# Causal attention stage: the 384-column and 128-column key-row scores share a PSUM slot, and the maxima are turned two pieces later

## The chip, the cores and the metric

The kernel runs on one core of a Trainium2 chip. Its time is the device time of one execution in microseconds (us); the median of the runs is what is compared. Five engines work beside one another, each through its own list of instructions in order: TensorE (PE, with its weight loads PEld), VectorE (DVE), ScalarE (ACT), GpSimd (POOL) and SyncE (SP, which only starts transfers here). Semaphores tie them together.

## The reference, cut to what matters

Two transformer layers run one after the other on x of shape (4, 1024, 128). The change touches only the attention of the second layer: 16 heads of 8, causal, with a recurrence beside it.

```python
scores = jnp.einsum('bhid,bhjd->bhij', q, k) * scale
causal_mask = jnp.triu(jnp.full((Ll, Ll), -10000.0, dtype=scores.dtype), 1)
attn = jax.nn.softmax(scores + causal_mask, axis=-1)
y_softmax = jnp.einsum('bhij,bhjd->bhid', attn, v)
...
state = retention * state + Gamma * hebbian          # the recurrence, one step per position
y_t = jnp.einsum('bhij,bhj->bhi', W_static + state, q_t)
...
y = alpha * y_softmax + (1.0 - alpha) * y_stp
```

## The kernel before

The causal stage works on 4 batches times 4 groups of 4 heads: 16 units `(b, g)`. The 1024 positions are 8 tiles of P = 128; BANK is 512 columns, one PSUM bank. A `ring` of three PSUM slots of two banks each (1024 columns) takes nearly every result of TensorE. Slots go round in the order of the items, and PE may fill one only when the item three before it has been read (`pe_wait_free`).

Each unit is computed in two passes.

- **M items (row maxima).** For each tile of queries, PE makes the scores with the queries on the partitions (L1280, and two small masking matmuls L1284 and L1287 where the tile is on the diagonal), and DVE reduces them to negated maxima (L1430). A unit has 20 such pieces. After the last one DVE joins two halves (L1434), and POOL splits the maxima into three bf16 parts with four small instructions (L1678, L1680, L1682, L1684).
- **S item (turned maxima).** PE transposes the parts (L1294) into a ring slot, ACT copies them (L1517), and SP starts four small transfers (L1606) that put them as extra rows under the queries, so that the key-row scores come out with the maximum already subtracted.
- **W items (key-row scores).** PE makes the scores with the keys on the partitions (L1309, masks L1313 and L1316), and ACT takes their exponential (L1530) from the ring slot into one of four buffers `c_probs`.
- **V items.** PE multiplies the exponentials by the values (L1337) into the accumulator `acc`, which is no ring slot. ACT copies it out at the end of a chunk (A item, L1536).

W and V go through `KEY_STEPS`: chunk c = 0 of 512 queries needs key tiles j = 0 to 3, chunk c = 1 needs j = 0 to 7. The last four tiles of a chunk lie on the diagonal, and leave 512, 384, 256 and 128 columns of queries. `score_pairs` says how the two pairs of heads share slots: a step of 512 or 384 columns takes two slots, one for each pair; a step of 256 or 128 columns takes one slot for both pairs. So a chunk takes 6 or 14 slots, a unit 20, the stage 320, with 320 exponentials: 14 of 1024 columns in a unit, 4 of 768 and 2 of 512.

`causal_order` writes the common order of all items. It keeps a model of when PE, ACT, DVE and the slots come free. M pieces of the next unit (`ahead`) are put before W and V items so that they lead by 9 to 19 W items, at a rate `ratio` = 21/20 of them (20 M and one S) to each W; they may be put earlier when the model says that this costs no wait. V of a step is put after the W items of the next step. The recurrence is a chain of side items, tied to the key steps (8 rounds j in a batch, 6 key steps for each): `kv` (POOL L1691), `scan` (DVE L1440), `scale` (ACT L1543), `read` (POOL L1703 and L1706). The preparation of the next batch and the finishing of the last one (`turn`, `q`, `k`, `v`, `gate1`, `gate2`, `vT`, `beta`, `att`, `tp`) are side items too; 19 of them a batch take ring slots.

Of the kernel before, what the change touches and what calls it, by code (L numbers as in the profile page):

```python
# [8 lines left out]
ACT = mybir.ActivationFunctionType  # L9
# [4 lines left out]
P = 128  # L14
# [106 lines left out]
def build(nc, x_in, packed, x_out, place, batches, T, known):  # L121
# [7 lines left out]
    with ctx:  # L129
# [764 lines left out]

        def score_pairs(c, j):
            cols = (c + 1) * BANK - max(c * BANK, j * P)
            return [(0, 1)] if 2 * cols <= BANK else [(0,), (1,)]

        KEY_STEPS = [(c, j) for c in range(HALVES) for j in range((c + 1) * BANK // P)]

# [111 lines left out]
        def causal_order():  # L1012
# [64 lines left out]
            def times(item):  # L1077
                if item[0] == "next":
                    return MOE_TIMES.get(item[1], (0, (("D", 1.1),), 0))
                if item[0] == "M":  # L1080
                    n, (_, a, c, _, per) = item[3], causal_pieces(item[3])[item[4]]
                    mask = 0.15 * per if c == (n + 1) * P else 0
                    return 0.00077 * per * (c - a) + mask, (("D", 0.16 + 0.00204 * per * (c - a)),), 1
                if item[0] in "WV":
                    c, j = item[3:5]
                    a = max(c * BANK, j * P)
                    cols = (c + 1) * BANK - a
                    if item[0] == "V":
                        return 0.00205 * cols, (), 0
                    n = len(score_pairs(c, j)[item[5]])  # L1090
                    return n * (0.00077 * cols + (0.15 if a == j * P else 0)), (("A", 0.17 + 0.00166 * n * cols),), 1
                return TIMES.get(item[0], (0, (), 0))
# [5 lines left out]
            def begin(item):  # L1098
                t = clock["P"]
                if times(item)[2]:  # L1100
                    t = max(t, free[0])
                return max(t, made[item[1:]]) if item[0] == "V" else t

            def put(item):
# [12 lines left out]
                if item[0] == "W":  # L1117
                    made[item[1:5]] = done + HOP

# [25 lines left out]
            for u in units:  # L1145
                for k, (c, j) in enumerate(KEY_STEPS):
                    for i in range(len(score_pairs(c, j))):
                        put_ahead(("W", *u, c, j, i))
                        put(("W", *u, c, j, i))
                        done += 1  # L1150
                        while sums:
                            put(sums.pop())

                    late.append(("V", *u, c, j))
                    if len(late) > 1:
                        item = late.pop(0)
                        put_ahead(item)
                        put(item)
                        if item[4] == (item[3] + 1) * BANK // P - 1:
                            sums.append(("A", *item[1:4]))  # L1160
# [14 lines left out]
        def causal():  # L1175
# [9 lines left out]
            chunk = lambda b, g, c: (b * GROUPS + g) * HALVES + c  # L1185
            first_query = lambda c, j: max(c * BANK, j * P)
            last_W = lambda b, g: ("W", b, g, *KEY_STEPS[-1], len(score_pairs(*KEY_STEPS[-1])) - 1)
            unit = lambda b, g: b * GROUPS + g
# [33 lines left out]
            def pe_program():  # L1222
# [3 lines left out]
                for item in order:  # L1226
# [70 lines left out]
                    elif kind == "W":  # L1297
# [3 lines left out]
                        pe.wait_ge(shift_signal(b, g, part), (b, g, part))  # L1301
                        a = first_query(c, j)
                        cols = (c + 1) * BANK - a
                        qs, ks = cq_stack[b % 2], ck_stack[b % 2]
                        diag = a == j * P
                        for k, pair in enumerate(score_pairs(c, j)[i]):
                            o = [ps[:, r * BANK + k * BANK // 2:r * BANK + k * BANK // 2 + cols] for r in range(2)]
                            for r in range(2):
                                mm = nc.tensor.matmul(o[r], ks[half(r, SHIFT), 2 * g + pair, j * P:(j + 1) * P],  # L1309
                                                      qs[half(r, SHIFT), 2 * g + pair, a:a + cols], start=True, stop=not diag)  # L1310
# [8 lines left out]
                    elif kind == "V":  # L1319
# [7 lines left out]
                        if j == 0 and ci >= 2:  # L1327
                            pe.wait_ge(c_copied, ci - 2)
                        shares = score_pairs(c, j)
                        pe.wait_ge(c_weights_made, ("W", *item[1:], len(shares) - 1))  # L1330
                        for i in range(2):
                            k = i if len(shares) > 1 else 0
                            weights = c_probs[w_index["W", b, g, c, j, k] % 4]
                            for r in range(2):
                                h = 2 * i + r
                                first = r * BANK + (i - k) * BANK // 2
                                mm = nc.tensor.matmul(  # L1337
                                    acc[ci % 2][32 * h:32 * h + HD + 1, a - c * BANK:BANK],
                                    c_values[b % 2][:, j, r * HEADS // 2 + 2 * g + i, :],
                                    weights[:, first:first + (c + 1) * BANK - a],  # L1340
                                    start=j == 0, stop=j == (c + 1) * BANK // P - 1, skip_group_check=True)
                        mm.then_inc(c_weighed.up(item), 1)
# [128 lines left out]
            def act_program():  # L1471
# [3 lines left out]
                for item in order:  # L1475
# [43 lines left out]
                    elif kind == "W":  # L1519
                        _, b, g, c, j, i = item  # L1520
                        wi = w_index[item]
                        cols = (c + 1) * BANK - first_query(c, j)
                        if len(score_pairs(c, j)) > 1:
                            view = lambda ap: ap[:, :].rearrange("p (r c) -> p r c", r=2)[:, :, 0:cols]
                        else:
                            view = lambda ap: ap[:, :].rearrange("p (r k c) -> p r k c", r=2, k=2)[:, :, :, 0:cols]
                        ac.wait_ge(c_key_scored, item)
                        if wi >= 4:
                            ac.wait_ge(c_weighed, ("V", *w_items[wi - 4][1:5]))
                        nc.scalar.activation(view(c_probs[wi % 4]), view(ps), ACT.Exp).then_inc(c_weights_made.up(item), 1)  # L1530
                    elif kind == "A":
                        _, b, g, c = item
                        ac.wait_ge(c_weighed, ("V", b, g, c, (c + 1) * BANK // P - 1))
                        if b:
# [1335 lines left out]
```

## Time and profile before

| | |
|---|---|
| median of 3 runs | 1893.22 us (1888.89 to 1899.77) |
| the profiled execution | 1901.14 us, span 1899.8 us |
| causal stage in it | from about 1030 to 1650 us of the span |
| busy in the stretch 1030 to 1650 | PE 505, DVE 483, ACT 404, POOL 319 us of 620 |
| pieces in the stage | 320 M, 320 W |

Each row of such a profile is one engine's busy time or one group of instructions. A bracket behind a row of the timeline is the time for which that engine sat idle before the instruction, and what ended it. PE's busy time has the latency of each matmul in it, so it is an upper value.

### The profile page before, as it was taken

How to read it: one execution, taken by the hardware profiler on the slowest of the kernel's cores; microseconds unless marked ns; L12 is line 12 of the kernel's file. 1: busy time of each engine (PE TensorE's matmuls, PEld its weight loads, DVE VectorE, ACT ScalarE, POOL GpSimd, SP SyncE). 2: the span in 40 equal slices, each digit the busy share in tenths (PEclk: the TensorE clock that was granted, in tenths of full speed). 3: DMA queues.
4: the chain of work that ended last, by engine and by line, in shares of the span. 5: the costliest groups of instructions: out<-in, count | busy, mean ns of one | idle time of the engine just before them, and what ended most of it. 6: DMA issues, size and time to landing. Idle time of an engine off the chain costs nothing. (4 is left out here: it accounts for less than half of the span.)

```text
span 1899.8 us, 45062 instructions
## 1 busy us (share of the span) xinstructions
PE 1656.2 (87%) x19472; PEld 1024.8 (54%) x19472; DVE 1276.2 (67%) x2059; ACT 1114.6 (59%) x1654; POOL 695.8 (37%) x508
## 2 busy tenths in 40 slices
PE   4588888999999999999997778888888888899999
PEld 2355555677677767776775233343343343466665
DVE  4566645667666666666765868877877886755664
ACT  2265567766676667667763366667766767533221
POOL 5212202444244434424443164555554564411100
PEclk7699898999999999999998699999998999999999
DMA  7674100000000000000014236236327323000000
GB/s 171 161 194 121 22 14 2 2 2 2 1 2 2 2 1 2 2 2 1 2 46 115 68 121 168 68 91 162 74 71 182 75 62 75 23 6 12 6 12 12
DMA packets 38748, 102.27 MB, mean 54 GB/s; under 512 B 3944, under 2 KB 12288, under 8 KB 35284
## 3 DMA queue, kind: packets, MB, share of 16 engines
q1 hardware_dynamic: 38548, 99.38, 20.6%
q8 instruction: 153, 2.51, 0.6%
q14 instruction: 47, 0.39, 0.1%
HBM read 67.12 MB, written 31.46 MB: 52 GB/s over the span
## 5 line engine op out<-in xcount | busy, mean ns | idle before, releaser
L1430 DVE TENSOR_REDUCE arena<-ring 128x2 f32<-128x1024 f32 (+2 forms) x320 | 342.1, 1110 | 87.8 <-PE ring L1287 61.9
L1530 ACT ACTIVATE arena<-ring 128x1024 f32<-128x1024 f32 (+1 forms) x320 | 291.2, 937 | 132.4 <-PE ring L1316 89.1
L1337 PE MATMUL accs<-arena 128*9 128x512 f32 (+3 forms) x1536 | 173.9, 526 | 2.7 <-ACT arena L1530 2.6
L1280 PE MATMUL ring<-arena 48*128 48x512 bf16 (+3 forms) x768 | 129.5, 349 | 40.7 <-DVE arena L1430 19.9
L1309 PE MATMUL ring<-arena 51*128 51x512 bf16 (+3 forms) x768 | 125.0, 344 | 45.4 <-DVE arena L1430 25.1
L2469 POOL TENSOR_TENSOR arena<-arena 128x1280 f32<-128x1280 f32 x28 | 65.3, 2332 | 266.6 <-PE accs L2239 235.2
L2453 POOL TENSOR_TENSOR arena<-arena 128x1024 f32<-128x1024 f32 x32 | 76.0, 2376 | 203.3 <-DVE arena L2329 203.3
L2461 POOL TENSOR_TENSOR arena<-arena 128x512 f32<-128x512 f32 x112 | 141.9, 1299 | 11.3 <-DVE arena L2310 11.3
L292 POOL TENSOR_SCALAR xn<-x,moments,rstd 128x128 f32<-128x128 f32 x88 | 70.5, 815 | 192.4 <-DVE rstd L263 174.2
L2736 ACT ACTIVATE arena<-ring 128x512 f32<-128x512 f32 x80 | 47.7, 597 | 147.3 <-PE ring L2591 140.5
L2696 DVE TENSOR_TENSOR arena<-arena,ring 128x512 f32<-128x512 f32 x80 | 55.0, 687 | 87.8 <-PE ring L2593 74.4
L1703 POOL TENSOR_TENSOR arena<-arena 128x1024 f32<-128x1024 f32 x28 | 65.9, 2353 | 128.6 <-ACT arena L1543 104.3
L1309 PEld LDWEIGHTS ring<-arena 51*128 51x128 bf16 x768 | 36.6, 95 | 138.9 <-DVE arena L1430 75.4
L2613 PEld LDWEIGHTS accs<-weights_large,arena 128*128 128x128 f32 x640 | 83.5, 192 | 27.1 <-issue 23.5
L2329 DVE TENSOR_TENSOR arena<-ring,arena 128x1024 f32<-128x1024 f32 x32 | 39.2, 1225 | 86.7 <-PE ring L2201 86.7
L1280 PEld LDWEIGHTS ring<-arena 48*128 48x128 bf16 x768 | 38.5, 96 | 109.1 <-DVE arena L1430 41.4
L623 DVE TENSOR_REDUCE arena<-ring 128x8 f32<-128x1024 f32 x51 | 61.7, 1220 | 46.3 <-PE ring L516 45.9
L2201 PE MATMUL ring<-arena 64*128 64x128 f32 x1024 | 91.1, 285 | 1.2 <-DVE arena L1955 1.1
L2003 ACT ACTIVATE arena<-ring 128x1024 f32<-128x1024 f32 x32 | 32.8, 1024 | 101.0 <-PE ring L1907 97.4
L2201 PEld LDWEIGHTS ring<-arena 64*128 64x128 f32 x1024 | 78.6, 187 | 21.8 <-issue 13.5
L2613 PE MATMUL accs<-weights_large,arena 128*128 128x128 f32 x640 | 84.5, 275 | 0.5 <-DVE arena L2701 0.5
L2413 ACT ACTIVATE arena<-arena 128x512 f32<-128x512 f32 x128 | 81.5, 707 | 0.0
(345 smaller groups left out, 4275.3 us busy)
## 6 DMA issues: line engine op xcount, KB each, us to landing
arena<-whole_k SPq DMA_DIRECT2D x32, 512.0 KB, 4.7
arena<-whole_q SPq DMA_DIRECT2D x32, 512.0 KB, 6.3
arena<-a_scratch_q SPq DMA_DIRECT2D x16, 384.0 KB, 7.3
arena<-a_scratch_k SPq DMA_DIRECT2D x16, 384.0 KB, 8.8
arena<-c_scratch_q SPq DMA_DIRECT2D x14, 384.0 KB, 8.0
arena<-c_scratch_k SPq DMA_DIRECT2D x14, 384.0 KB, 11.5
a_scratch_k<-arena SPq DMA_DIRECT2D x8, 512.0 KB, 4.1
c_scratch_k<-arena SPq DMA_DIRECT2D x8, 512.0 KB, 4.1
```

Of the source, the lines that this page charges most:

```text
L292: nc.gpsimd.tensor_scalar(xn[n % 4][:, :], x[:, b * NT + n, :], moments[:, n, 0:1], rstd[:, 3, n:n + 1], ALU.subtract, ALU.mult).then_inc( ...
L1280: mm = nc.tensor.matmul(o[r], qs[half(r, SCORE), pair, n * P:(n + 1) * P], ks[half(r, SCORE), pair, a:c], start=True, stop=not diag)
L1309: mm = nc.tensor.matmul(o[r], ks[half(r, SHIFT), 2 * g + pair, j * P:(j + 1) * P], qs[half(r, SHIFT), 2 * g + pair, a:a + cols], start=Tru ...
L1337: mm = nc.tensor.matmul(acc[ci % 2][32 * h:32 * h + HD + 1, a - c * BANK:BANK], c_values[b % 2][:, j, r * HEADS // 2 + 2 * g + i, :], weig ...
L1430: nc.vector.tensor_reduce(dst, src, AX.X, ALU.max, negate=True).then_inc(c_max_taken.up(item), 1)
L1530: nc.scalar.activation(view(c_probs[wi % 4]), view(ps), ACT.Exp).then_inc(c_weights_made.up(item), 1)
L1703: nc.gpsimd.tensor_tensor(sq[:, :], sk[:, :], sq[:, :], ALU.mult).then_inc(c_y_step.up((b, j)), 1)
L2201: mm = nc.tensor.matmul(ps[:, r * BANK + p * P:r * BANK + (p + 1) * P], k_[t % 2][half(r), p * P:(p + 1) * P], q_[t % 2][half(r), p * P:(p ...
L2413: nc.scalar.activation(v5[t % 2][:, 1 + r, :], v5[t % 2][:, 0, :], ACT.Copy, scale=route_hot[t // NT % 2][:, t % NT, r:r + 1]).then_inc(v_ ...
L2453: nc.gpsimd.tensor_tensor(masked[0][:, :], masked[0][:, :], masked[1][:, :], ALU.add).then_inc(gla_joined.up(t), 1)
L2461: nc.gpsimd.tensor_tensor(pair_cols(q2m[t % 2][:, r, :]), pair_cols(q2[t % 2][:, :]), hot_b[:, r * P:(r + 1) * P].unsqueeze(1).to_broadcas ...
L2613: mm = nc.tensor.matmul(moe_total[:, n * P:(n + 1) * P], hid[i % 3][:, n * P:(n + 1) * P], w("d_down", f * P, (f + 1) * P), start=f == 0 a ...
```

## The change

It touches three things.

- The scores of key tile `last - 3` (384 columns) and of the last key tile `last - 1` (128 columns) of a chunk go into the same slot, one slot for each pair of heads: 384 columns at 0 and 128 at 384 of each bank. The last key tile has no slot of its own any more. Every slot is full, so every exponential has 1024 columns. The matmuls and masks are the same as before.
- The steps of a chunk now go `..., last - 1, last - 2`. Step `last - 1` issues no W. Its V item follows V of `last - 3` directly, behind the W of `last - 2`, and V of `last - 2` comes last. Side items that were tied to the third and fourth step of a chunk's tail keep their step numbers.
- The S item is inserted after four M pieces of the next unit, not after two.

```diff
-        def score_pairs(c, j):
-            cols = (c + 1) * BANK - max(c * BANK, j * P)
-            return [(0, 1)] if 2 * cols <= BANK else [(0,), (1,)]
-        KEY_STEPS = [(c, j) for c in range(HALVES) for j in range((c + 1) * BANK // P)]
+        def chunk_steps(c):
+            last = (c + 1) * BANK // P
+            return [*range(last - 2), last - 1, last - 2]
+        KEY_STEPS = [(c, j) for c in range(HALVES) for j in chunk_steps(c)]
+        def score_blocks(c, j):
+            last = (c + 1) * BANK // P
+            if j == last - 1:
+                return []
+            if j == last - 2:
+                return [[(0, j, 0), (1, j, BANK // 2)]]
+            if j == last - 3:
+                return [[(pair, j, 0), (pair, last - 1, BANK - P)] for pair in range(2)]
+            return [[(pair, j, 0)] for pair in range(2)]
+        def blocks_of(c, j):
+            found = {pair: (step, i, a) for step in chunk_steps(c) for i, blocks in enumerate(score_blocks(c, step))
+                     for pair, tile, a in blocks if tile == j}
+            return [found[pair] for pair in range(2)]
...
-                    rows.insert(2, ("S", *units[u - 1], 0))
+                    rows.insert(4, ("S", *units[u - 1], 0))
...
-            ratio = (len(maxima(units[1])) + 1) / sum(len(score_pairs(*k)) for k in KEY_STEPS)
+            ratio = (len(maxima(units[1])) + 1) / sum(len(score_blocks(*k)) for k in KEY_STEPS)
...
-                    if len(late) > 1:
+                    while scores and len(late) > 1:
                         item = late.pop(0)
                         put_ahead(item)
                         put(item)
-                        if item[4] == (item[3] + 1) * BANK // P - 1:
+                        if item[4] == last_step(item[3]):
                             sums.append(("A", *item[1:4]))
...
-                        for k, pair in enumerate(score_pairs(c, j)[i]):
-                            o = [ps[:, r * BANK + k * BANK // 2:r * BANK + k * BANK // 2 + cols] for r in range(2)]
+                        for pair, tile, at in score_blocks(c, j)[i]:
+                            a = first_query(c, tile)
+                            cols = (c + 1) * BANK - a
+                            diag = a == tile * P
+                            o = [ps[:, r * BANK + at:r * BANK + at + cols] for r in range(2)]
...
-                            ac.wait_ge(c_weighed, ("V", *w_items[wi - 4][1:5]))
-                        nc.scalar.activation(view(c_probs[wi % 4]), view(ps), ACT.Exp).then_inc(c_weights_made.up(item), 1)
+                            *former, step, k = w_items[wi - 4][1:]
+                            ac.wait_ge(c_weighed, ("V", *former, score_blocks(former[2], step)[k][-1][1]))
+                        nc.scalar.activation(c_probs[wi % 4][:, :], ps[:, :], ACT.Exp).then_inc(c_weights_made.up(item), 1)
```

## Rows read from the trace of the kernel before

**Rows 1.** The page, busy time of each engine over the whole span.

```profile
PE 1656.2 (87%) x19472; PEld 1024.8 (54%) x19472; DVE 1276.2 (67%) x2059; ACT 1114.6 (59%) x1654; POOL 695.8 (37%) x508
```

**Rows 2.** Busy by stretch: length, then PE, PEld, DVE, ACT, POOL, clock, DMA share, GB/s.

```profile
1030.00:1650.00 620.00, 505.29 (x5750) 215.78 (x5751) 483.20 (x555) 404.19 (x472) 319.44 (x218) 0.93 0.39 99
...
1319.48:1348.41 28.93, 23.64 (x328) 8.93 (x328) 26.10 (x23) 22.16 (x26) 16.96 (x10) 1.00 0.37 89
...
1348.41:1391.95 43.54, 35.77 (x410) 17.02 (x412) 34.11 (x53) 28.95 (x34) 20.43 (x13) 1.00 0.21 50
```

**Rows 3.** The chain that ended last, by line, in the stretch 1093 to 1603.

```profile
by line: DVE arena L1430 24.0%; PE accs L1337 14.2%; DVE arena L1440 7.7%; issue 7.0%; PE ring L1309 6.0%; PE ring L1280 5.9%; ACT arena L1530 4.6%; PE ring L928 1.9%; POOL arena L1691 1.8%; PE ring L1348 1.8%; DMA c_scratch_q<-arena 1.5%; 
```

**Rows 4.** Groups by shape in 1030 to 1650: busy us, mean ns, idle before.

```profile
L1430 DVE TENSOR_REDUCE arena<-ring 128x2 f32<-128x1024 f32 x192 | 228.3, 1217 | 50.4 <-PE ring L1287 26.1 <-PE ring L1280 23.2
L1530 ACT ACTIVATE arena<-ring 128x1024 f32<-128x1024 f32 x224 | 222.4, 1022 | 100.9 <-PE ring L1316 58.5 <-PE ring L1309 41.9
...
L1530 ACT ACTIVATE arena<-ring 128x768 f32<-128x768 f32 x64 | 51.2, 812 | 17.2 <-PE ring L1316 16.7
...
L1530 ACT ACTIVATE arena<-ring 128x512 f32<-128x512 f32 x32 | 19.1, 595 | 14.3 <-PE ring L1316 13.9
```

**Rows 5.** Line L1430: what its engine sat idle for (us, times).

```profile
  PE ring L1287: 61.9, 60
  PE ring L1280: 23.2, 23
```

**Rows 6.** ACT timeline: three of the 15 full-width S copies.

```profile
1093.83 1.01 ACT L1517 ACTIVATE arena<-ring 12x1024 bf16<-12x1024 f32 x1 [1.33 <-PE ring L1294]
...
1199.63 1.01 ACT L1517 ACTIVATE arena<-ring 12x1024 bf16<-12x1024 f32 x1 [0.16 <-PE ring L1294]
...
1602.92 1.01 ACT L1517 ACTIVATE arena<-ring 12x1024 bf16<-12x1024 f32 x1 [1.57 <-PE ring L1294]
```

**Rows 7.** DVE timeline of a unit without side jobs, its idle gaps.

```profile
1470.15 0.96 DVE L1430 TENSOR_REDUCE arena<-ring 128x2 f32<-128x768 f32 x1 [0.52 <-PE ring L1287]
1471.70 5.54 DVE L1430 TENSOR_REDUCE arena<-ring 128x2 f32<-128x768 f32 x5 [0.59 <-PE ring L1287]
1477.91 1.82 DVE L1430 TENSOR_REDUCE arena<-ring 128x4 f32<-128x512 f32 x2 [0.68 <-PE ring L1287]
1480.48 3.49 DVE L1430 TENSOR_REDUCE arena<-ring 128x2 f32<-128x1024 f32 x3 [0.74 <-PE ring L1280]
```

**Rows 8.** POOL and DVE timeline around a split, and another unit's L1682.

```profile
1163.10 2.36 POOL L1691 TENSOR_TENSOR arena<-arena 128x1024 f32<-128x1024 f32 x1
...
1166.02 2.28 DVE L1440 TENSOR_TENSOR_SCAN arena<-arena 128x1024 f32<-128x1024 f32 x1
...
1166.19 2.14 POOL L1682 CAST arena<-arena 128x32 bf16<-128x32 f32 x1
...
1601.55 0.24 POOL L1682 CAST arena<-arena 128x32 bf16<-128x32 f32 x1
```

**Rows 9.** Line L1294 in 1080 to 1600: idle of PE until (us, times).

```profile
  POOL arena L1684: 4.3, 4
```

**Rows 10.** A slow stretch behind an S: busy by engine and clock, timeline.

```profile
1168.50:1173.00 4.50, 4.14 (x35) 1.40 (x37) 2.15 (x3) 4.00 (x5) 0.53 (x2) 0.65 0.51 128
...
1170.18 1.90 PE L1337 MATMUL accs<-arena 128*9 128x512 f32 x8
...
1172.71 5.54 DVE L1430 TENSOR_REDUCE arena<-ring 128x2 f32<-128x768 f32 x5 [1.82 <-PE ring L1287]
...
1175.39 1.05 PE L1337 MATMUL accs<-arena 128*9 128x512 f32 x8
```

**Rows 11.** PE timeline: V of 384 columns and V of 128 columns.

```profile
1184.82 0.83 PE L1337 MATMUL accs<-arena 128*9 128x384 f32 x8
...
1189.83 0.41 PE L1337 MATMUL accs<-arena 128*9 128x128 f32 x8
```

**Rows 12.** ACT timeline near the stage's end: the copy of turned beta.

```profile
1637.76 1.02 ACT L1507 ACTIVATE arena<-ring 128x1024 f32<-128x1024 f32 x1 [4.90 <-PE ring L1254]
```

More of the change, by code:

```diff
@@ L892, in stack_signal @@
             return ((c_stack_there[0, 0], (0, 0)), (c_stack_there[0, 1], (0, 1)), (c_stack_there[1, 0], (0, 2)))[min(g, 2)]
-        def score_pairs(c, j):
-            cols = (c + 1) * BANK - max(c * BANK, j * P)
-            return [(0, 1)] if 2 * cols <= BANK else [(0,), (1,)]
-        KEY_STEPS = [(c, j) for c in range(HALVES) for j in range((c + 1) * BANK // P)]
+        def chunk_steps(c):
+            last = (c + 1) * BANK // P
+            return [*range(last - 2), last - 1, last - 2]
+        KEY_STEPS = [(c, j) for c in range(HALVES) for j in chunk_steps(c)]
+        last_step = lambda c: chunk_steps(c)[-1]
+        first_query = lambda c, j: max(c * BANK, j * P)
+        def score_blocks(c, j):
[11 more added lines that the diff above has]
+            return [found[pair] for pair in range(2)]
         CAUSAL_FIRST = {
@@ L1083, in times @@
                     return 0.00077 * per * (c - a) + mask, (("D", 0.16 + 0.00204 * per * (c - a)),), 1
-                if item[0] in "WV":
+                if item[0] == "V":
                     c, j = item[3:5]
[L1086 to L1091, printed above, removed]
+                    return 0.00205 * ((c + 1) * BANK - first_query(c, j)), (), 0
+                if item[0] == "W":
+                    c, j, i = item[3:6]
+                    masks = sum(tile * P >= c * BANK for _, tile, _ in score_blocks(c, j)[i])
+                    return 0.00077 * BANK + 0.15 * masks, (("A", 0.17 + 0.00166 * BANK),), 1
                 return TIMES.get(item[0], (0, (), 0))
@@ L1101, in begin @@
                     t = max(t, free[0])
-                return max(t, made[item[1:]]) if item[0] == "V" else t
+                return max(t, *(made[item[1:4] + (step, i)] for step, i, _ in blocks_of(*item[3:5]))) if item[0] == "V" else t
             def put(item):
@@ L1117, in put @@
                 if item[0] == "W":
-                    made[item[1:5]] = done + HOP
+                    made[item[1:]] = done + HOP
             first, second = ([i for i in maxima(units[0]) if (i[3] < NT // 2) == early] for early in (True, False))
@@ L1146, in causal_order @@
                 for k, (c, j) in enumerate(KEY_STEPS):
-                    for i in range(len(score_pairs(c, j))):
+                    scores = score_blocks(c, j)
+                    for i in range(len(scores)):
                         put_ahead(("W", *u, c, j, i))
@@ L1185, in causal @@
             chunk = lambda b, g, c: (b * GROUPS + g) * HALVES + c
-            first_query = lambda c, j: max(c * BANK, j * P)
-            last_W = lambda b, g: ("W", b, g, *KEY_STEPS[-1], len(score_pairs(*KEY_STEPS[-1])) - 1)
+            last_W = lambda b, g: ("W", b, g, *KEY_STEPS[-1], len(score_blocks(*KEY_STEPS[-1])) - 1)
             unit = lambda b, g: b * GROUPS + g
@@ L1301, in pe_program @@
                         pe.wait_ge(shift_signal(b, g, part), (b, g, part))
-                        a = first_query(c, j)
-                        cols = (c + 1) * BANK - a
                         qs, ks = cq_stack[b % 2], ck_stack[b % 2]
-                        diag = a == j * P
-                        for k, pair in enumerate(score_pairs(c, j)[i]):
-                            o = [ps[:, r * BANK + k * BANK // 2:r * BANK + k * BANK // 2 + cols] for r in range(2)]
+                        for pair, tile, at in score_blocks(c, j)[i]:
[3 more added lines that the diff above has]
+                            o = [ps[:, r * BANK + at:r * BANK + at + cols] for r in range(2)]
                             for r in range(2):
-                                mm = nc.tensor.matmul(o[r], ks[half(r, SHIFT), 2 * g + pair, j * P:(j + 1) * P],
+                                mm = nc.tensor.matmul(o[r], ks[half(r, SHIFT), 2 * g + pair, tile * P:(tile + 1) * P],
                                                       qs[half(r, SHIFT), 2 * g + pair, a:a + cols], start=True, stop=not diag)
@@ L1328, in pe_program @@
                             pe.wait_ge(c_copied, ci - 2)
[L1329 to L1333, printed above, removed]
+                        for step, i, _ in blocks_of(c, j):
+                            pe.wait_ge(c_weights_made, ("W", b, g, c, step, i))
+                        for pair, (step, i, at) in enumerate(blocks_of(c, j)):
+                            weights = c_probs[w_index["W", b, g, c, step, i] % 4]
                             for r in range(2):
-                                h = 2 * i + r
-                                first = r * BANK + (i - k) * BANK // 2
+                                h = 2 * pair + r
+                                first = r * BANK + at
                                 mm = nc.tensor.matmul(
                                     acc[ci % 2][32 * h:32 * h + HD + 1, a - c * BANK:BANK],
-                                    c_values[b % 2][:, j, r * HEADS // 2 + 2 * g + i, :],
+                                    c_values[b % 2][:, j, r * HEADS // 2 + 2 * g + pair, :],
                                     weights[:, first:first + (c + 1) * BANK - a],
-                                    start=j == 0, stop=j == (c + 1) * BANK // P - 1, skip_group_check=True)
+                                    start=j == 0, stop=j == last_step(c), skip_group_check=True)
                         mm.then_inc(c_weighed.up(item), 1)
```

7 lines of the change are left out of this document (1 added, 6 removed).

## The prediction, made before the changed kernel was run

> **What bounds the kernel now.** I read the page first, then the stage by stretches, then the chain of waits inside it, and last the timelines of single units. Over the whole span PE is the busiest engine [rows 1], but that is an average over four layers of work; the change touches only the causal stage, so only the stage counts. There PE shows 505 us of 620 busy, DVE 483, ACT 404 [rows 2]. PE's share holds the latency of each matmul, so DVE is as near to its limit. The chain of waits agrees: of 510 us in the middle of the stage the row-max reductions take 24%, the V matmuls 14%, the scan 8%, and the exponential only 4.6% [rows 3].
>
> The reader is to see two kinds of unit. A plain unit, without side jobs, takes 28.93 us with DVE busy for 26.10 of them [rows 2]. Its gaps on DVE of over half a us are 0.52, 0.59, 0.68 and 0.74, together 2.53 us of the 2.8 that DVE has free [rows 7]; nothing can give more there than these. A unit with side jobs takes up to 43.54 us with DVE busy for 34.11 [rows 2]: no engine is full, and the three ring slots and the common order set the pace. Between the S copies at 1093.83 and 1602.92 [rows 6] lie 14 units; four are plain like the one at 1319, ten have side jobs. In front of its reductions DVE waits 85.1 us in all for scores, in 83 gaps [rows 5].
>
> **The W slots.** The change takes two of 20 W slots from each unit, 32 in all. PE has the same matmuls, masks and columns: nothing saved, nothing added. ACT loses two exponentials of 595 ns and makes four 210 ns longer (1022 against 812 ns) [rows 4]: 1190 less 840 is 350 ns a unit, 5.6 us over 16 units. ACT has a third of its time free, so these 5.6 us are not the gain by themselves. What may pay is the turn of the slot. I price a slot by time: from the S copy at 1199.63 to that at 1348.41 [rows 2, 6] a batch passes in 148.78 us. It has 4 times 41 ring pieces and 19 side pieces, 183 in all. Without its plain unit (28.93 us, 41 pieces) there are 119.85 us for 142 pieces, 0.84 us a slot. A removed slot's work does not vanish: it makes two others longer by 0.21 us of ACT each, 0.42 us. What is left is 0.42 us a slot, 0.85 a unit, 8.5 us in ten units. The bounds: below it 0, if DVE or the V matmuls fill every turn that comes free (a loss is the rivals' matter); above it the full price, 10 x 2 x 0.84 = 17 us.
>
> In the four plain units DVE sets the time. Here the removed slot helps PE and ACT, which already wait. Of the gaps, 0.52 and 0.59 follow the S piece, which takes one of three slots between two M pieces; they move with it. I take 0.4 us a unit out of the other 1.42, so 1.6 us; the bounds are 0 and 1.42 x 4 = 5.7.
>
> The first unit is a ramp and the last one ends on the recurrence: ACT waits 4.90 us for the turned beta [rows 12], and PE had to wait for POOL's round of the recurrence before that. Fewer exponentials don't shorten that round. I give both nothing; if that cover is gone, they give at most 0.85 each.
>
> **The S piece two later.** Fourteen S items move. PE waited at them for POOL's split 4 times, 4.3 us in all [rows 9]; that wait can go whole or not at all. In the unit at 1166 the split is slow because L1682 takes 2.14 us, where it takes 0.24 in the last unit: in the first case it runs beside DVE's scan of 2.28 us, and ends with it [rows 8]. The next reduction stands behind the same scan, so DVE would have been late anyway. So most of PE's wait is covered, and I take 1.4 of the 4.3 us; bounds 0 and 4.3. The clock is part of it: behind the S at 1168, where PE had stood still, the mean granted clock of 4.5 us is 0.65, so a good part of them ran at 1.2 instead of 2.4 GHz; one V group takes 1.90 us where 1.05 is usual, and DVE has a gap of 1.82 us [rows 10] where others have 0.59 [rows 7]. That is inside the 1.4.
>
> A rule speaks against this part. The Trainium skill (GPSIMD Engine Reference, section 8, Key points) says that POOL shares its SBUF interfaces with DVE and is held up by DVE instructions with two SBUF inputs; a scan is one. By that rule, the trace agrees (2.14 against 0.24 us). It makes the split end with the scan wherever S stands, so the moved S would be worth 0 and the sum 10.1 us instead of 11.5; by the bare row of PE's waits it would be 14.4.
>
> What is queued behind: on SP the four small transfers of S move back with it, by two M pieces, some 2.4 us; the fetches for the recurrence stand behind them, but they wait for POOL anyway. The W items that need S come over seven ring pieces after it, by the lead of nine W items; at 0.71 us a piece and the W and V between, they don't meet it. The other new wait, ACT's exponential on V of tile `last - 1`, is behind a V that PE has already passed when the buffer comes round.
>
> **The sum.** 8.5 + 1.6 + 1.4 = 11.5 us. The profiled execution took 1901.14 us with a span of 1899.8; it lies 7.9 us above the median, so I take the difference from both: 1889.6 us for this execution, 1881.7 us for the median, which I round to 1882.
>
> **Rivals.**
>
> *Nothing to gain.* DVE sets the pace in more than the plain units, and the turns that come free are filled by waiting. For it: DVE at 78% of the whole stage [rows 2] and 24% of the chain [rows 3]. Against: a gap in every third or fourth reduction [rows 5], and 9.4 us free in the long unit [rows 2]. Time: 1893.2 less 0 to 4, so 1891.
>
> *More than expected.* Each removed slot brings its full price, 17 us in ten units and 5.7 in the plain ones, and the S waits go: 4.3. That is 27 us, 1866. For it: ACT idles 14.3 us before 32 short exponentials and 100.9 before 224 full ones, 0.45 us each in both [rows 4], so a slot costs a turn whatever is in it. Against: DVE's 90% in plain units.
>
> *Slower: the scan comes too early.* The side items keep their step numbers, but a chunk's tail now has one W less. The scan of every second round stands in the tail of chunk 0, three steps after its `kv`. In the unit at 1163 POOL's `kv` ends at 1165.46 and the scan starts at 1166.02 [rows 8]: a slack of 0.56 us. Between scale and scan there were 6 W and, at 21/20, 6.3 M; now 5 W and, at 21/18, 5.8 M. If that moves the scan up by one reduction of 1.22 us, DVE stands for 0.66 us; over some 15 units 10 us, which eats the gain. That is where it decides. If it moves by two, it is 1.88 us each, 28 us, less 11.5: 1910; the middle of both is 1901 to 1902. Against it: the M pieces have lead enough, and half a piece is less than the slack.
>
> *The order is worse by chance.* V of 384 and V of 128 columns now run together, 0.83 + 0.41 = 1.24 us [rows 11] in which PE fills no slot, about one reduction of 1.22 [rows 4]. Where no M piece is put between them and DVE has one piece in hand, it loses the 0.41 at each of 32 tails: 13 us, and the time is about 1895.
>
> **How the numbers follow.** Forecast, with its own range 1874 to 1889: 0.46. Nothing to gain: 0.22. More than expected: 0.12. The early scan: 0.14. The V run: 0.06. About 0.5%, 9.5 us, is what a measurement of this kernel can tell from no change. Three quarters of the forecast lie beyond it, 0.35; with the larger gain that is 0.47 for faster. Same: the last quarter of the forecast, 0.20 of nothing to gain and half of the V run: 0.34. Slower: the early scan, the other half of the V run, and 0.02 of nothing to gain: 0.19. The range of eight in ten goes from the larger gain to the milder half of the early scan: 1866 to 1900. It leaves out a scan that is early by two pieces, and gains of over 27 us.
>
> **What would show it in the changed profile.** L1530 has one form, 288 times at about 1022 ns. DVE's idle time before L1430 falls from 85 us [rows 5] by some 8 to 12; the batch period falls from 148.8 us to about 146; plain units stay between 28 and 28.9 us. PE's waits for L1684 are gone in the middle of the stage. The early scan would show as DVE idle before L1440 with POOL L1691 as the releaser, where before there was a single such gap. The V run would show as gaps before L1430 right behind L1337 of 128 columns. I am wrong if units with side jobs don't get shorter, or if the plain ones get shorter by more than 1 us.

## The result and the profile after

The change makes the kernel slower by 0.6%. Median of the changed kernel 1904.37 us (1900.5 to 1911.36, 10 runs), of the kernel before 1892.66 us (1887.65 to 1899.77, 10 runs); the ratio is 1.0062, 95% interval 1.0041 to 1.0084. The forecast was 1882 with a range up to 1900: the sign is wrong, and the time lies outside.

The profiled execution of the changed kernel took 1901.77 us with a span of 1900.3. The first view is the busy time by stretch: the stage from the first M matmul to the last V, and then four units, each from one S copy to the next. Columns as in [rows 2].

```profile
1020.40:1645.80 625.40, 502.56 (x5725) 219.71 (x5726) 484.78 (x548) 398.86 (x435) 316.17 (x216) 0.90 0.38 98
...
1280.00:1319.40 39.40, 32.74 (x348) 12.36 (x348) 26.04 (x26) 27.67 (x30) 20.85 (x13) 0.83 0.78 175
1319.40:1350.50 31.10, 25.91 (x334) 9.93 (x330) 25.77 (x23) 21.90 (x24) 16.97 (x11) 0.89 0.27 70
1434.70:1469.80 35.10, 28.41 (x348) 11.91 (x348) 26.01 (x26) 27.41 (x30) 20.82 (x13) 0.95 0.82 191
1469.80:1498.60 28.80, 23.18 (x334) 9.35 (x330) 25.78 (x23) 21.91 (x24) 17.00 (x11) 1.00 0.33 83
```

The same view of the kernel before:

```profile
1031.50:1644.50 613.00, 499.75 (x5726) 212.48 (x5727) 478.76 (x548) 400.99 (x468) 314.16 (x216) 0.92 0.40 99
```

A second execution of the kernel before, `before_again`, gives 612.6 us. So the stage grew by 12.4 us, and the medians by 11.7: the loss is in the stage. The profiled execution of before had been a long one (1901.14, above all ten that were timed); what was long there was the part ahead of the stage, 1031.5 us against 1020.4 here.

The reader is to see three things. ACT's work in the stage fell by 2.1 us and DVE's rose by 6.0, 4.0 of it in the 32 scans (77.8 us against 73.8); PE's rose by 2.8; on each engine the rest of the 12 us is waiting. Why some scans are longer stands in the last section. Second, the plain unit of two different batches (the rows of 31.10 and 28.80 us) holds the same instructions in the same written order and takes that much at a granted clock of 0.89 and 1.00. A plain unit took 28.93 before [rows 2]: at full clock the changed kernel neither gains nor loses there. Third, the loss is not spread evenly. Between the S copies of the same units the parts of the stage take 112.8, 154.1, 148.1 and 106.3 us, where they took 105.8, 148.8, 150.2 and 104.3: the two earlier parts lose 12.3 us, and the third is shorter than before.

Next the groups of the same stretch by shape, what DVE sat idle for in front of the reductions, and what PE waited for at the fourteen S items that were moved (those in 1080 to 1600, as in [rows 9]).

```profile
L1546 ACT ACTIVATE arena<-ring 128x1024 f32<-128x1024 f32 x288 | 287.5, 1021 | 133.9 <-PE ring L1337 81.0 <-PE ring L1330 52.0
L1460 DVE TENSOR_TENSOR_SCAN arena<-arena 128x1024 f32<-128x1024 f32 x32 | 77.8, 2431 | 5.7 <-POOL arena L1707 5.5
```
```profile
  PE ring L1308: 57.0, 54
  PE ring L1301: 28.4, 26
```
```profile
  ACT arena L999: 2.7, 4
  issue: 2.1, 5
  DVE arena L1450: 1.0, 4
```

The exponential (now L1546) has one form, 288 times at 1021 ns, and ACT works 5.2 us less on it (5.6 were worked out). But it sits idle 133.9 us in front of it: the three forms of before add to 100.9 + 17.2 + 14.3 = 132.4 [rows 4]. DVE's idle time in front of the reductions (now L1450) is 57.0 + 28.4 = 85.4 us, where it was 85.1 [rows 5]. The two waits that the slots were priced on are as long as they were.

The wait that the S move was priced on did go away. In front of the fourteen moved S items PE waited 4.3 us for POOL's split [rows 9]; now not at all. (Over the whole kernel 4.6 us are left of 9.4, at the three S items that did not move.) With its other releasers PE's idle time in front of these fourteen fell from 20.9 to 5.8 us, and the kernel is slower even so.

The S copies on ACT's timeline, the three that bound two batches:

```profile
1196.44 1.00 ACT L1537 ACTIVATE arena<-ring 12x1024 bf16<-12x1024 f32 x1
...
1350.51 1.00 ACT L1537 ACTIVATE arena<-ring 12x1024 bf16<-12x1024 f32 x1
...
1498.62 1.00 ACT L1537 ACTIVATE arena<-ring 12x1024 bf16<-12x1024 f32 x1
```

The batch that took 148.78 us before takes 154.07 us, and the next one 148.11 (150.20 before). The first unit of the two batches differs by a few items; the other three are written alike. The two pairs of units shown above, 39.4 + 31.1 us against 35.1 + 28.8, differ by 6.6; the two units ahead of them differ by 0.7 the other way.

Where most of the 4.3 us of the first of these units arise can be read in one place of both. ACT's timeline at `gate1` in the one batch and in the next:

```profile
1287.48 1.11 ACT L1509 ACTIVATE arena<-ring,weights_small 64x1024 f32<-64x1024 f32 x1 [2.88 <-PE ring L1261]
...
1439.28 1.11 ACT L1509 ACTIVATE arena<-ring,weights_small 64x1024 f32<-64x1024 f32 x1 [0.51 <-PE ring L1261]
```

PE's timeline, the V group of 512 columns behind it, in the one batch and in the next:

```profile
1291.36 1.89 PE L1357 MATMUL accs<-arena 128*9 128x512 f32 x8
...
1442.94 1.04 PE L1357 MATMUL accs<-arena 128*9 128x512 f32 x8
```

And the busy time and clock of the two 15 us:

```profile
1282.00:1297.00 15.00, 12.89 (x88) 3.06 (x88) 8.33 (x8) 9.74 (x9) 8.29 (x4) 0.72 0.56 174
1436.80:1451.80 15.00, 12.77 (x144) 5.58 (x140) 9.88 (x11) 11.32 (x12) 8.18 (x4) 1.00 0.70 208
```

PE is busy for 12.9 and 12.8 us of them, yet finishes 88 matmuls in the one and 144 in the other: part of the first ran at 1.2 GHz, all of the second at 2.4. A V group takes 1.89 us instead of 1.04, and ACT waits 2.88 us where it waited 0.51. Just before, behind the S copy, PE had stood still for 1.72 us in both batches; the granted clock of the 2 us around it is 0.57 (1280 to 1282) in the one and stays at 1.00 (1434.8 to 1436.8) in the other. Counted from the S copy, the V group of the view starts 3.1 us later in the first batch. The order alone does not fix the time; how it falls onto the clock does too.

### The profile page after: what moved, and what is told of

Its sections match the earlier page's. It is cut to its first block and busy times, and to the rows that moved or that the text cites. A ratio compares the mean times of both kernels' runs of the same rounds, so it can differ in the third digit from the quotient of the medians.

```text
span 1900.3 us, 44984 instructions
## 1 busy us (share of the span) xinstructions
PE 1649.1 (87%) x19451; PEld 1025.4 (54%) x19472; DVE 1281.4 (67%) x2059; ACT 1112.0 (59%) x1622; POOL 696.9 (37%) x508
## 5 line engine op out<-in xcount | busy, mean ns | idle before, releaser
L1450 DVE TENSOR_REDUCE arena<-ring 128x2 f32<-128x1024 f32 (+2 forms) x320 | 341.0, 1109 | 87.2 <-PE ring L1308 57.0
L1546 ACT ACTIVATE arena<-ring 128x1024 f32<-128x1024 f32 x288 | 287.5, 1021 | 133.9 <-PE ring L1337 81.0
L292 POOL TENSOR_SCALAR xn<-x,moments,rstd 128x128 f32<-128x128 f32 x88 | 76.2, 880 | 187.4 <-DVE rstd L263 173.9
L1719 POOL TENSOR_TENSOR arena<-arena 128x1024 f32<-128x1024 f32 x28 | 65.9, 2354 | 120.9 <-ACT arena L1559 106.3
L2019 ACT ACTIVATE arena<-ring 128x1024 f32<-128x1024 f32 x32 | 32.8, 1024 | 100.1 <-PE ring L1923 96.5
L1460 DVE TENSOR_TENSOR_SCAN arena<-arena 128x1024 f32<-128x1024 f32 x32 | 77.8, 2431 | 5.7 <-POOL arena L1707 5.5
```

The source lines that it names most:

```text
L292: nc.gpsimd.tensor_scalar(xn[n % 4][:, :], x[:, b * NT + n, :], moments[:, n, 0:1], rstd[:, 3, n:n + 1], ALU.subtract, ALU.mult).then_inc( ...
L1450: nc.vector.tensor_reduce(dst, src, AX.X, ALU.max, negate=True).then_inc(c_max_taken.up(item), 1)
L1460: nc.vector.tensor_tensor_scan(sk[:, :], c_retain[:, j:j + 1].to_broadcast([P, T]), sk[:, :], 0.0, ALU.mult, ALU.add).then_inc(c_state_mad ...
L1546: nc.scalar.activation(c_probs[wi % 4][:, :], ps[:, :], ACT.Exp).then_inc(c_weights_made.up(item), 1)
L1719: nc.gpsimd.tensor_tensor(sq[:, :], sk[:, :], sq[:, :], ALU.mult).then_inc(c_y_step.up((b, j)), 1)
```

## The experiments

Each ratio is to the kernel before, measured beside it; in brackets its 95% interval. Labels in **bold**.

**The parts of the change, one by one.** First the slots without the move of S, the move of S without the slots, the slots in the old written order, and the kernel before once more.

**pack_s2**, the changed kernel with S behind two pieces:

```diff
-                    rows.insert(4, ("S", *units[u - 1], 0))
+                    rows.insert(2, ("S", *units[u - 1], 0))
```

> The changed kernel with S back behind two M pieces: packed slots and their planned order alone. If the packing with its new order is the cause (theory 1), the time stays 8 to 13 us above the kernel before, about 1901 to 1906. If the later S is the cause (theory 2), it falls to 1890 +- 4. If the two only lose together, 1893 to 1898.

Measured: 1909.14 us, ratio 1.0098 (1.0077 to 1.0120).

**s4_only**, the kernel before with the reverse of that edit:

> The kernel before with S behind four M pieces instead of two, nothing else. Theory 1 (packing and its order) expects 1889 to 1895, no difference to be measured. Theory 2 (the later S) expects 1900 to 1906.

Measured: 1892.61 us, ratio 1.0001 (0.9987 to 1.0015).

**pack_old_order**, the slots of the change, but the order written by the planner of before, with the last tile's own W items struck out and the last two V items exchanged; S behind two:

```diff
+            packed_order = []
+            for item in order:
+                if item[0] in "WV" and len(item) > 4:
+                    c, j = item[3:5]
+                    last = (c + 1) * BANK // P
+                    if item[0] == "W" and j == last - 1:
+                        continue
+                    if item[0] == "V" and j >= last - 2:
+                        item = ("V", *item[1:4], 2 * last - 3 - j)
+                packed_order.append(item)
+            return packed_order
```

> Packed slots, but the order of all items is the one that the planner of the kernel before writes: the W items of the last key tile are struck out, and the V items of the last two key tiles change places; S stands behind two M pieces. If the new order is what costs (theory 1a: side items run together in the empty steps, M pieces lead by less), this is 1883 to 1893, as the blind forecast had it for the slots. If the packed slots themselves or the V run cost (theory 1b), it is 1900 to 1906 as the changed kernel.

Measured: 1890.01 us, ratio 0.9991 (0.9973 to 1.0009).

**before_again**, the kernel before, unchanged:

> The kernel before once more under its own label, unchanged: the ratio must hold 1.0 in its interval; its profile gives a second length of the causal stage. If the stage's length is fixed by the order, it is 613 us within 3 us again; if the clock in the stage is a matter of chance, it differs by 5 to 10 us with another mean clock in the same stretches.

Measured: 1890.55 us, ratio 0.9995 (0.9978 to 1.0012).

What follows: the fuller slots cost nothing and bring nothing that can be measured. S two pieces later brings nothing in the old order that can be measured, though in `s4_only` too PE's waits for the split at the moved S items are gone, and its idle time in front of them is 6.7 us instead of 20.9. The loss appears only where the planner has written a new order around the new slots: `pack_s2` and `pack_old_order` have the same slots and S behind two, and are at 1.0098 and 0.9991. In the new order the later S seems to help, 1.0062 against 1.0098, but these two intervals overlap.

**What the new order does at a chunk's tail.** The written orders of the third batch's second unit, chunk 0's tail, before and after (`M7a` is the first piece of query tile 7, `W1.0b` chunk 1, key tile 0, second slot):

```
before       W0.2a V0.1 /v_0 W0.3a M7a V0.2 /mid_q /scan_2 W1.0a W1.0b M7b V0.3
pack_old     W0.2a V0.1 /v_0       M7a V0.3 /mid_q /scan_2 W1.0a W1.0b M7b V0.2
after   /v_0 W0.2a M7c V0.1 V0.3       /mid_q /scan_2 W1.0a W1.0b M7d V0.2
```

The step without W has lost its place: its side items stand directly behind those of the step before, its V directly behind another V, and the M pieces stand elsewhere. Three kernels put the two tail edits one by one into `pack_old_order`, whose M and S pieces stay in place.

**old_order_bunched**: side items of the dropped step directly behind those of the step before it.

```diff
+                    moved = [i for i in packed_order if side_step.get(i) == (*u, c, last - 2)]
...
+                    packed_order[at:at] = moved
```

> Packed slots in the old planner's order (1890.0 before), with one thing more: the side items that stood behind the dropped W of a chunk's tail now stand directly behind those of the step before, as in the changed kernel (q with v, scan with vT and scale, two att together). If this bunching costs (theory A), 1896 to 1902. If it doesn't, 1888 to 1892.

Measured: 1897.85 us, ratio 1.0029 (1.0015 to 1.0042).

**old_order_vrun**: V of the last tile directly behind V of the third last.

```diff
+                    packed_order.remove(("V", *u, c, last - 1))
+                    packed_order.insert(packed_order.index(("V", *u, c, last - 3)) + 1, ("V", *u, c, last - 1))
```

> Packed slots in the old planner's order, with V of the last key tile directly behind V of the 384-column tile, and no M piece between them. If the V run costs (theory B, the last rival of the blind forecast), 1896 to 1903. If it doesn't, 1888 to 1892.

Measured: 1899.73 us, ratio 1.0032 (1.0009 to 1.0055).

**old_order_new_tail**: both edits.

> Both: the tail of each chunk has the shape that the changed kernel gives it, and only the places of the M and S pieces are still those of the old planner. If where the M pieces stand is what costs (theory C), this stays at 1888 to 1893, and the changed kernel's loss of 11.7 us is theirs alone. If the tail is the cause (A and B together), 1899 to 1906.

Measured: 1897.42 us, ratio 1.0029 (1.0013 to 1.0045).

**spread_sides**: the changed kernel, with the side items of the step without W held back to between the two V items.

```diff
+                        while held:
+                            put(held.pop(0))
...
-                        put(item)
+                        if scores:
+                            put(item)
+                        else:
+                            held.append(item)
```

> The changed kernel, with the side items of the empty step put between the two V items instead of directly behind those of the step before. Its planner sees that and moves M pieces by one here and there. Theory A expects 1892 to 1897 (the loss mostly gone). Theories B and C expect 1901 to 1907, no difference from the changed kernel.

Measured: 1901.07 us, ratio 1.0051 (1.0032 to 1.0071).

Each tail edit costs about 0.3% (0.4% against `pack_old_order`), and both together no more than one. That is a part of the loss. Spreading the side items in the changed kernel gives back 0.1%, inside the intervals, so this alone doesn't undo it.

**Is it the clock alone, or a lead of the M pieces that is too small?** Two kernels double PE's off-diagonal M matmuls of 512 columns, so that PE idles less; one raises the least lead; and one tries S behind four in the old order.

**before_twice** and **after_twice**:

```diff
-                            for r in range(2):
+                            for r in 2 * (0, 1) if not diag else (0, 1):
```

> The kernel before, with the two 512-column score matmuls of every M piece off the diagonal made twice into the same place (128 pieces, same result): 0.2 us more PE work each, 28 us in all, most of it in time that PE stands still. It keeps TensorE busier. If the clock is what turns small waits into microseconds (theory D), the time at the low clock in the stage falls below 80 us and the kernel is no more than 5 us slower than before: 1888 to 1898. If PE's work sets the time, 1905 to 1920.

> The changed kernel with the same doubled matmuls. Theory D (the changed order loses because TensorE falls to its low clock more often) expects it within 5 us of before_twice. Theory C (the places of the M pieces cost waits at either clock) expects it still 9 to 14 us above before_twice.

Measured: 1894.52 us, ratio 1.0013 (0.9995 to 1.0031), and 1919.24 us, ratio 1.0128 (1.0108 to 1.0147). The gap between the two orders is 24.7 us with the added work, where it was 11.7. The added work is free in the old order and dear in the new one: a PE that idled too much is not the reason by itself.

**lead_12**:

```diff
-            least, most = 9, 19
+            least, most = 12, 19
```

> The changed kernel with the planner's least lead of the M pieces raised from 9 to 12 W items. If the M pieces come too late for the W items in the changed order (theory C1), 1892 to 1898. If the lead does nothing and any reshuffle of the order is as good or bad as another (theory C2), 1898 to 1910.

Measured: 1928.84 us, ratio 1.0186 (1.0168 to 1.0204). More lead makes it much worse.

**old_order_s4**, `pack_old_order` with S behind four pieces:

> Packed slots in the old planner's order, S behind four M pieces: the two parts of the change without the new order. Theory C expects 1888 to 1893, as each part alone (1890.0 and 1892.6). If packing and the later S hurt each other, 1897 or more.

Measured: 1890.6 us, ratio 0.9986 (0.9972 to 1.0000).

**The lead itself, and the tail at S behind four.** The lead is counted in W items, and there are fewer of them: 9 at 21/20 were 9.45 pieces, 9 at 21/18 are 10.5. **lead_8** and **lead_6** are the changed kernel with `least` 8 and 6; **lead_8_spread** is `spread_sides` with 8; **new_tail_s4** is `old_order_new_tail` with S behind four.

> The changed kernel with the least lead of the M pieces at 8 W items, not 9. At 21/18 that is 9.33 pieces, close to the 9.45 that the kernel before has (9 at 21/20); with 9 it is 10.5. A larger lead, 12, gave 1928.8 us against 1904.4. Theory 'the grown lead is the loss': the time falls by the part that 1.05 pieces of lead cost, to 1892 to 1897. Theory 'any other placement of the M and S pieces costs': the order is again a new one, and the time stays at 1900 to 1910. Theory 'the M pieces come too late': above 1906, with more idle time in front of the exponentials.

Measured: 1909.61 us, ratio 1.0070 (1.0044 to 1.0096).

> The changed kernel with the least lead at 6 W items, 7.0 pieces. Grown lead: as good as a lead of 8 or better, at most 1897. Any other placement: 1900 to 1915, without order between leads of 6, 8 and 9. If the scores of a unit then come before its turned maxima are ready, PE waits at the first W of a unit and the time is above 1905; that would show as PE idle on the S transfers.

Measured: 1932.12 us, ratio 1.0191 (1.0164 to 1.0218).

> The changed kernel with a least lead of 8 and with the side items of the step without W held back, so that they stand between the two V items. Bunching of side items costs on its own: 2 to 5 us below the lead of 8 alone. Bunching is no cost here: within 2 us of it. Both theories of the placement together leave 1891 to 1895.

Measured: 1895.99 us, ratio 1.0001 (0.9978 to 1.0025).

> The slots of the change in the old order of the M pieces, S behind four M pieces, and the tail of the change: side items of the step without W directly behind those of the step before, V of the last tile directly behind V of the third last. It differs from the changed kernel only in where M and S pieces stand. Theory 'the placement of the M and S pieces carries the rest': 1896 to 1898, about 7 us below the changed kernel. Theory 'the tail together with the later S is the loss': 1902 or more, as the changed kernel.

Measured: 1902.56 us, ratio 1.0038 (1.0020 to 1.0056). Beside these four kernels the kernel before had a median of 1895.97 us, some 3 us more than beside the others, so the ratio is what counts.

In the changed order a smaller lead gives back nothing: 8 is at 1.0070, 9 at 1.0062, and 6 and 12 are both far worse. The tail costs at S behind four too, with intervals that don't touch: 0.9986 without and 1.0038 with the new tail, 0.5%. From there to the changed kernel's 1.0062 only the places of M and S differ; that is 0.24%, and the intervals overlap.

One kernel in a newly planned order loses nothing, `lead_8_spread`, and it changes the reading of all the others. With the M and S items struck out, the written orders of `spread_sides` and `lead_8_spread` are those of `old_order_s4`, item for item: holding the side items back gives the old tail. In the same way `lead_8` and the changed kernel are `new_tail_s4`. So six kernels with the same slots, S behind four in all, differ in only two things:

| | M and S where the old planner had them | newly planned, lead 8 | newly planned, lead 9 |
|---|---|---|---|
| old tail | 0.9986 (0.9972 to 1.0000), `old_order_s4` | 1.0001 (0.9978 to 1.0025), `lead_8_spread` | 1.0051 (1.0032 to 1.0071), `spread_sides` |
| new tail | 1.0038 (1.0020 to 1.0056), `new_tail_s4` | 1.0070 (1.0044 to 1.0096), `lead_8` | 1.0062 (1.0041 to 1.0084), the changed kernel |

The two faults don't add up; each is enough. With the old tail the places of the M pieces at a lead of 9 cost 0.65%, and going from 9 to 8 gives back 0.5%, both with intervals that don't touch. With the new tail there is little left for them to cost, and a lead of 8 gives nothing. To undo the loss both had to be mended: 0.7% from `lead_8` to `lead_8_spread`. The written orders also say how far the M pieces moved. With the old tail they stand on average 0.3 W items earlier than in `old_order_s4` at a lead of 8, and 1.7 earlier at 9. With the new tail, against `new_tail_s4`, they stand 0.5 later at 8, 0.9 earlier at 9, 3.2 earlier at 12 (1.0186) and 2.1 later at 6 (1.0191). The further from where the old planner had them, the dearer, with one pair out of line: 0.5 later costs as much as 0.9 earlier. No kernel was made to test that distance by itself.

The plain unit of each, the same one of a batch, first `lead_8`:

```profile
1480.60:1511.00 30.40, 24.71 (x330) 9.73 (x328) 25.90 (x23) 21.96 (x25) 16.25 (x11) 0.94 0.29 72
```

and `lead_8_spread`:

```profile
1466.10:1494.70 28.60, 23.95 (x336) 9.54 (x334) 25.56 (x23) 22.98 (x24) 16.64 (x12) 1.00 0.33 79
```

This unit has no preparation items, only a round of the recurrence, and differs by 1.8 us. In it ACT stands 0.97 us for the scan before `scale` in `lead_8` and 0.21 us in `lead_8_spread`, with all exponentials queued behind `scale`; later a V group takes 1.89 us in `lead_8` (start 1503.60), and in `lead_8_spread` none takes over 1.05. That is one place and no general cause: over the whole stage ACT waits 8.8 us for the scan in the one and 8.3 in the other, twelve times in each.

## Why the prediction was wrong

**The step that failed most** is one that has no term: the sum held the places of all other pieces fixed. A dropped W item shifts the M pieces, since both the rate and the lead are counted in W items, and the step without W drops its side items and its V onto the step before. With the same slots and S behind two, the planner's new order is at 1.0098 (1.0077 to 1.0120) and the old one at 0.9991 (0.9973 to 1.0009). With S behind four it is 1.0062 (1.0041 to 1.0084) against 0.9986 (0.9972 to 1.0000). That is the loss, and in place of a term of nothing it is 0.8 to 1.1%, 14 to 19 us. I named half of it as rivals. The V run was priced as up to 13 us if there is no M piece between and DVE has one in hand; alone it measured 0.3%, some 6 us, the milder half. The scan that comes too early was priced as DVE idling for POOL's `kv`, some fifteen times; it did so for 5.5 us in two waits, against 2.3 in one before, so that form of it is refuted, and that its 1901 to 1902 lies near the measured time is luck. Three scans do stand longer for POOL, 4.0 us in all, but behind the preparation's subtraction and not behind `kv`, and they do so in `lead_8_spread` as well, 3.35 us each, which loses nothing. Side items behind one another cost 0.3% alone; on which engine that falls was not shown.

**The price of a slot** is the term of the sum that failed: 8.5 us for the slots beside side jobs and 1.6 for the plain units. `pack_old_order` has the slots and keeps the order: 1890.01 us beside 1890.55 of `before_again`. So the 10.1 us measured as 0.5, and against the kernel before as 1.7, with 95% bounds of about 5 gained and 2 lost. "0.84 us a slot" was a mean of time over slots, not what one of them holds up. The turns that came free were filled by waiting, as in the rival with nothing to gain: DVE's idle time in front of the reductions, 85.1 us before, is 90.1 in `pack_old_order`.

**S two later** was taken as 1.4 us, and nothing of it can be seen: with the old slots 1.0001 (0.9987 to 1.0015) and with the new ones 1890.6 us against 1890.01. The intervals are as wide as the term, so 1.4 us is not excluded. What failed is the row that it came from. The wait for the split went whole, 4.3 us in four to none, in the changed kernel and in `s4_only` alike, and that was worth nothing that can be measured: PE's wait at S was covered. The caution gave the right worth, 0, for another reason than its own. The split's first cast still ends with a scan in four units of the changed kernel (it takes 2.17 us there), but S, two pieces later, no longer stands for it. In the new order the move may be worth 0.36%, with intervals that overlap.

**Parts that held.** ACT's saving of 5.2 us, which was not to be the gain by itself; the single form of the exponential; PE's waits for the split, gone in the middle of the stage; and the plain unit of 28.8 us at full clock (28 to 28.9 were forecast). The batch period was to fall to 146 us; the one that was read rose to 154.07, the next one is 148.11. DVE's idle time in front of the reductions was to fall by 8 to 12 us and stayed at 85.4.

**What stays open.** That the new order is the loss is shown, and that its tail and its places of the M pieces are each enough for most of it. How either of them turns into microseconds is not: no wait was found that is long in every bad order and short in every good one. The clock carries a part of the time (6.6 us between two pairs of units in the same order), but whether it comes first or follows from the waits is not shown: no run held it fixed. The doubled matmuls made the gap larger.

No version beats the kernel before by more than its interval. The best, `old_order_s4`, is at 0.9986 (0.9972 to 1.0000).

## What to carry to other kernels

Where a planner writes the common order of all engines, an edit to one item is an edit to the place of every other. Price it by replaying the old order with only that item changed, and look at what the planner does to the rest as a second change of its own: here the first was worth nothing and the second 0.8 to 1.1%. A step that loses its last paced item loses its spacing: give its side items and its accumulating matmuls a place, or they land on those of the neighbour. Where two faults are each enough, mending one of them shows nothing; try both together before either is cleared. And a mean time over slots in a stretch where no engine is full is not the price of a slot. Nor is a wait that goes away a gain: PE's idle time in front of the moved S items fell from 20.9 to 6.7 us in `s4_only`, and the time stayed.

## What the runs showed of the hardware

The same instructions in the same order took 70.5 us in one batch and 63.9 in the next of one execution, at granted clocks of 0.83 and 0.89 against 0.95 and 1.00. Summed over whole stages the clock goes the same way: 0.92 where the stage takes 613 us, 0.90 where it takes 625. Two stage rows of kernels with the same slots, S behind four in both, `old_order_s4` and `new_tail_s4`:

```profile
1023.50:1634.80 611.30, 497.96 (x5725) 213.68 (x5726) 478.19 (x548) 397.68 (x435) 301.98 (x216) 0.93 0.40 100
```
```profile
1021.50:1654.00 632.50, 515.08 (x5725) 225.31 (x5726) 473.95 (x548) 398.19 (x435) 308.29 (x216) 0.88 0.39 96
```

The same 5725 matmuls are busy for 17 us more at 0.88. (This execution of `new_tail_s4` took 1909.73 us, 7.2 above its median, so that the 21 us between the two stages overstate the mean difference.)

A scan on DVE that starts while POOL is inside a long instruction takes longer. Of the 32 scans of the changed kernel three take 3.85 to 3.94 us where the usual one takes 2.28; the longest, and what POOL did then:

```profile
1109.91 3.94 DVE L1460 TENSOR_TENSOR_SCAN arena<-arena 128x1024 f32<-128x1024 f32 x1
```
```profile
1109.57 2.14 POOL L1665 TENSOR_TENSOR arena<-arena 128x1024 f32<-128x1024 f32 x1
```

POOL's instruction ends at 1111.71, 1.8 us after the scan's start, and the scan is 1.66 us longer than usual. The two longest scans before, 2.72 and 2.73 us, each start 1.55 us into the same POOL instruction of 2.13 us, so 0.57 of it is left, and they are 0.45 longer than usual. Where POOL's instruction starts behind the scan, the scan takes its 2.28 us and POOL is the one that is held up, as at [rows 8]. The Trainium skill (GPSIMD Engine Reference, section 8, Key points) says that POOL shares its SBUF interfaces with DVE and contends with DVE instructions that have two SBUF inputs. By that rule, the trace agrees; it also shows that either engine can be the one held up.
